# The first 128 tokens of block 0 sent ahead in a four-stage transformer kernel, with the table of steps laid anew

## The reference

```python
x = x + attn(ln(x))    # 16 heads of 8 dims over 1024 keys; + input; LayerNorm with gamma, beta
x = x + ffn(ln(x))     # ternary weights: silu(x W1) * (x W2), two 512x512 GELU layers, then W3
x = x + gla(ln(x))     # gated linear attention: h = h * exp(gk) + k v^T, o = q h over T
x = x + zones(ln(x))   # router takes 3 of 8 expert FFNs (128 -> 512 -> 128) per batch
...
Q = x @ wq + bq; K = x @ wk + bk; V = x @ wv + bv
Q = Q.reshape(B * H, S, D); K = K.reshape(B * H, S, D); V = V.reshape(B * H, S, D)
attn = softmax(einsum('bqd,bkd->bqk', Q, K) / sqrt(D))
```

## Time and profile before

| | us |
|---|---|
| median of 3 runs (1034.36 to 1039.66) | 1035.55 |
| the profiled execution: its time | 1037.2 |
| the profiled execution: its span | 1034.9 |
| PE busy | 966.3 (93%) |
| ACT busy | 813.3 (79%) |
| DVE busy | 720.5 (70%) |
| POOL busy | 356.4 (34%) |
| first exponential (ACT L909) starts at | 28.18 |

### The profile page before, as it was taken

One profiled execution on the slowest core, in us unless ns is written; L12 is line 12 of the kernel. 1 busy time (PEld: TensorE's weight loads), 2 busy tenths in 40 slices (PEclk: granted clock), 3 DMA queues, 4 the chain that ended last, 5 costly groups with the idle time before them and its releaser, 6 DMA issues.

```text
span 1034.9 us, 16677 instructions
## 1 busy us (share of the span) xinstructions
PE 966.3 (93%) x5859; PEld 454.0 (44%) x5859; DVE 720.5 (70%) x1276; ACT 813.3 (79%) x1058; POOL 356.4 (34%) x309
## 2 busy tenths in 40 slices
PE   3999999999999999999999998999899999999998
PEld 1232235333533452346233533453347666566666
DVE  5223855567488778777888887688699998997300
ACT  0899888988889989999899898989976485644542
POOL 1000102114322435343625342534554465546100
PEclk8899999999999999999999999999999999999999
DMA  6855244065216533651266136412342322252020
GB/s 158 194 145 139 72 122 116 32 141 148 62 61 166 134 81 92 147 146 58 62 157 171 53 93 179 128 43 75 92 105 82 97 84 82 74 145 68 12 71 21
DMA packets 140998, 106.26 MB, mean 103 GB/s; under 512 B 92848, under 2 KB 107984, under 8 KB 140880
## 3 DMA queue, kind: packets, MB, share of 16 engines
q1 hardware_dynamic: 135984, 102.78, 37.3%
q10 hardware_dynamic: 4896, 1.87, 0.7%
HBM read 75.25 MB, written 29.36 MB: 101 GB/s over the span
## 4 chain that ended last, share of the span: by engine, by line
PE 47%; ACT 16%; DVE 16%; issue 11%; DMA 4%; POOL 4%; SPq 1%; ACTq 0%; DVEq 0%; POOLq 0%
PE PS L1488 14%; ACT R L909 9%; PE PS L1451 9%; PE PS L1535 7%; DVE R L1264 4%; DVE R L1255 4%; PE PS L1662 4%; DMA R<-VD 3%; ACT L883 3%; PE PS L1650 3%; PE PS L1575 2%; PE PS L1597 2%; PE PS L1606 1%; POOL R L854 1%; DVE RB L1220 1%
## 5 line engine op out<-in xcount | busy, mean ns | idle before, releaser
L909 ACT ACTIVATE R<-PS 128x1024 f32<-128x1024 f32 x512 | 487.2, 1042 | 55.9 <-PE PS L1451 54.2
L1488 PE MATMUL PS<-R 128*32 128x512 f32 x2048 | 293.5, 611 | 1.0 <-DVE R L1208 0.9
L854 POOL TENSOR_TENSOR R<-R 128x512 f32<-128x512 f32 x128 | 189.8, 1489 | 185.5 <-ACT R L985 126.0
L1451 PE MATMUL PS<-RA 32*128 32x512 f32 x1024 | 181.3, 500 | 29.0 <-ACT R L909 23.4
L1264 DVE TENSOR_TENSOR_SCAN R<-R 128x512 f32<-128x512 f32 x128 | 186.0, 1453 | 2.3
L1451 PEld LDWEIGHTS PS<-RA 32*128 32x128 f32 x1024 | 70.6, 183 | 255.3 <-ACT R L909 164.4
L1535 PE MATMUL PS<-RB,WR 128*128 128x512 f32 x640 | 175.7, 416 | 5.3 <-POOL RB L840 2.7
L1535 PEld LDWEIGHTS PS<-RB,WR 128*128 128x128 f32 x640 | 115.3, 189 | 69.0 <-issue 29.5
L883 ACT ACT_TABLE_LOAD x84 | 107.8, 1283 | 35.6 <-PE PS L1535 12.8
L1255 DVE TENSOR_TENSOR R<-R 128x512 f32<-128x512 f32 x128 | 118.5, 926 | 22.7 <-DMA R<-VD 18.5
L840 POOL TENSOR_TENSOR RB<-R,RB 128x512 fp32r<-128x512 f32 x48 | 74.9, 1560 | 164.6 <-DVE RB L1220 164.6
(11 more groups left out here) (127 smaller groups left out, 856.6 us busy)
## 6 DMA issues: line engine op xcount, KB each, us to landing
R<-VD SPq DMA_DIRECT2D x128, 256.0 KB, 4.1
RA<-QD SPq DMA_DIRECT2D x64, 256.0 KB, 4.4
QD<-RA SPq DMA_DIRECT2D x56, 256.0 KB, 3.9
RA<-QD SPq DMA_DIRECT2D x64, 128.0 KB, 4.3
OD<-R SPq DMA_DIRECT2D x32, 256.0 KB, 2.1
R<-OD SPq DMA_DIRECT2D x128, 32.0 KB, 2.5
R<-in_Wa SPq DMA_DIRECT2D x12, 256.0 KB, 3.7
R<-in_Wb SPq DMA_DIRECT2D x12, 256.0 KB, 4.2
```

Source lines behind the costliest of these rows:

```text
L854: pool.tensor_tensor(st, st, Qc, ALU.mult).then_inc(S["qh"], 1)
L909: act.activation(PR[u % 4], bank(2 * s, 1024), ACT.Exp, scale=SC).then_inc(S["exp"], 1)
L1451: op = pe.matmul(bank(2 * s + h), exact(KS[k][p:p + 32, 128 * j:128 * j + 128]), exact(QS[k][p:p + 32, :]), start=True, stop=stop)
L1488: op = pe.matmul(bank(ob)[c:c + 32, :], VAF[b % 2][:, at:at + 32], PR[u % 4][:, 512 * h:512 * h + 512], start=(j == 0), stop=(j == 7), til ...
```

## The change

Block 0 is treated in two parts, `(0, 0, 1)`, its first 128 tokens, and `(0, 1, 4)`, the other 384. x comes in two DMAs accordingly. The first part's K goes out by SP, its Q by ACT's DMA queue, and the first pair's keys are read by SP and its queries by ACT. The weights wA and the bias bA are asked for by ACT (in two halves), ahead of bv, gsel and block 1's x; the x of blocks 2 to 7 is asked for by SP after pair 2. For all blocks, `hi` is rounded straight from PSUM with the bias (DVE L1153; by ACT L937 for block 0's Q) and `lo` is formed straight from PSUM (L1157), so there is no Qf, one DVE instruction less, and the bank is given back after `lo`; the magnitude is taken of `hi`, and the limit is lowered by 2^-9 for that. PE's `values` waits for wA's second half (bv_in). POOL's `shift` waits for its own last instruction instead of a semaphore. The steps of block 1 no longer stand ahead of the first scores, and the string is another one, of the same length and with the same count of each letter.

```diff
-    "qqqqwxxxxxxxxxxxqxxxxxxlxxxxxxxxxxxxxxxwxwxxwxlxxxxxxwxxxfxxxqxxwfxwxxlxxwqqxwxxwxxxxxlxxwxxxxxfwxxx"
+    "xxxxxxxxxxxxqxxwxqxxqxxxxqxxxxxxwxxwxxxlxxfwxxxwqxxxxxxxxxwxwqxxlxxwxxxqxlqwxxxxxfxxxlwxxxwwfxxpxxxx"
...
     def start(self):
-        e = self.norm_in(0)
-        self.add("pads", 0)
-        self.add("turn_in", 0, 1, e)
-        self.add("split", 0, 1, 2)
-        self.add("keep", 0, 1, 0, 1)
-        self.add("split", 0, 0, 3)
-        self.add("keep", 0, 0, 0, 1)
-        self.add("load_pair", 0)
+        first, rest = (0, 0, 1), (0, 1, 4)
+        for k in range(2):
+            self.add("pads", k)
+        e = {}
+        n = self.stats("q", "X", first, ("x_in0", 16))
+        e[first] = self.apply("q", "XN", "X", first, n)
+        n = self.stats("q", "X", rest, ("x_rest", 16))
+        self.add("turn_in", first, 1, e[first])
+        e[rest] = self.apply("q", "XN", "X", rest, n)
+        self.add("split", first, 1, 2)
+        self.add("split", first, 0, 3)
+        self.add("first_out", 1)
+        self.add("first_out", 0)
+        self.add("turn_in", rest, 0, e[rest])
+        self.add("split", rest, 1, 4)
+        self.add("split", rest, 0, 5)
+        self.add("first_pair", 1)
+        self.add("first_pair", 0)
+        self.add("values", 0, 1)
+        self.add("flag", 0, 2)
         for w in (1, 0):
             self.add("keep", 0, w, 1, 4)
         for n in (1, 2):
             self.add("load_pair", n)
-        self.add("values", 0, 4)
-        self.add("flag", 0, 5)
-        self.add("pads", 1)
+        self.add("inputs")
         self.add("late_loads")
-        self.add("attend")
...
+        def keep_first(engine, need, w, landed):
+            need.wait_ge("qk_parts", split_no(0, 0, w))
+            for i in range(2):
+                for copy in range(2):
+                    engine.dma_start(place(0, w, 0, 1, i, copy), words(Qp[w][:, i, 0:128])).then_inc(S[landed], 16)
...
-            sp.dma_start(xblock(0), x_v[:, 0:4, :]).then_inc(S["x_in0"], 16)
-            sp.dma_start(wA[:, :, :], io["wA"]).then_inc(S["small_in"], 16)
-            sp.dma_start(bA[:, :], io["bA"]).then_inc(S["small_in"], 16)
+            sp.dma_start(X[:, 0:1, :], x_v[:, 0:1, :]).then_inc(S["x_in0"], 16)
+            sp.dma_start(X[:, 1:4, :], x_v[:, 1:4, :]).then_inc(S["x_rest"], 16)
...
+            def first_out(w):
+                if w:
+                    keep_first(sp, need, w, "k_out0")
+
+            def first_pair(w):
+                if w:
+                    need.wait_ge("k_out0", 64)
+                    keys(0, 0, "pair_in0")
+
+            def inputs():
+                for b in range(2, NBLK):
+                    sp.dma_start(xblock(b), x_v[:, 4 * b:4 * b + 4, :]).then_inc(S["x_in%d" % b], 16)
...
             def shift(k, n):
                 i = LNS[k]
-                need.wait_ge("rstd_" + k, n)
...
+            act.dma_start(wA[:, 0:2, :], io["wA"][:, 0:2, :]).then_inc(S["small_in"], 16)
+            act.dma_start(bA[:, :], io["bA"]).then_inc(S["small_in"], 16)
+            act.dma_start(wA[:, 2:4, :], io["wA"][:, 2:4, :]).then_inc(S["bv_in"], 16)
             for c in range(2):
                 act.dma_start(bv2[64 * c:64 * c + 64, :, :],
                               bass.AP(io["bv"].tensor, 8 * c, [[0, 64], [16, 8], [1, 8]])).then_inc(S["bv_in"], 16)
             act.dma_start(gsel[:, :], io["gsel"]).then_inc(S["ones"], 16)
-            for b in range(1, NBLK):
-                act.dma_start(xblock(b), x_v[:, 4 * b:4 * b + 4, :]).then_inc(S["x_in%d" % b], 16)
+            act.dma_start(xblock(1), x_v[:, 4:8, :]).then_inc(S["x_in1"], 16)
...
+            def split(part, w, bk):
+                b, i0, i1 = part
+                if b == 0 and w == 0:
+                    need.wait_ge("qk_ps", split_no(b, i0, w))
+                    need.wait_ge("small_in", 32)
+                    act.activation(exact(Qp[0][:, 0, 128 * i0:128 * i1]), bank(bk)[:, 128 * i0:128 * i1], ACT.Identity,
+                                   bias=bA[:, 0:1]).then_inc(S["q_hi"], 1)
+
+            def first_out(w):
+                if w == 0:
+                    keep_first(act, need, w, "q_out0")
+
+            def first_pair(w):
+                if w == 0:
+                    need.wait_ge("q_out0", 64)
+                    queries(act, 0, 0, "pair_in0")
...
-            def split(b, w, bk):
-                n = split_no(b, w)
-                hi, lo = Qp[w][:, 0, :], Qp[w][:, 1, :]
+            def turn_in(part, bk, e):
+                b, i0, i1 = part
+                need.wait_ge("xt_ps", turn_no(b, i0))
+                dve.tensor_copy(xtblock(b)[:, 128 * i0:128 * i1], bank(bk)[:, 128 * i0:128 * i1]).then_inc(S["xt"], 1)
+
+            def split(part, w, bk):
+                b, i0, i1 = part
+                n = split_no(b, i0, w)
+                ps = bank(bk)[:, 128 * i0:128 * i1]
+                hi, lo = (exact(Qp[w][:, i, 128 * i0:128 * i1]) for i in range(2))
                 need.wait_ge("qk_ps", n)
                 need.wait_ge("small_in", 32)
-                if n > 1:
-                    need.wait_ge("amax", n - 1)
-                    need.wait_ge("qk_parts", n - 1)
-                dve.tensor_scalar(Qf, bank(bk), bA[:, w:w + 1], None, ALU.add).then_inc(S["qk_f"], 1)
-                need.wait_ge("qk_f", n)
                 if b:
                     need.wait_ge("k_out" if w else "q_out", 64 * b)
-                    need.wait_ge("qk_out0", 128)
-                own.step(dve.tensor_copy(exact(hi), Qf))
-                own.settle()
-                dve.tensor_tensor(exact(lo), Qf, exact(hi), ALU.subtract).then_inc(S["qk_parts"], 1)
-                dve.tensor_reduce(am[:, 2 * b + w:2 * b + w + 1], Qf, AX.X, ALU.max,
+                    need.wait_ge("k_out0" if w else "q_out0", 64)
+                    need.wait_ge("amax", 2 * b - w)
+                if b or w:
+                    own.step(dve.tensor_scalar(hi, ps, bA[:, w:w + 1], None, ALU.add))
+                    own.settle()
+                else:
+                    need.wait_ge("q_hi", 2 if i0 else 1)
+                dve.scalar_tensor_tensor(lo, ps, bA[:, w:w + 1], hi, ALU.add, ALU.subtract).then_inc(S["qk_parts"], 1)
+                if b:
+                    largest(b, w)
+                elif i0 and w == 0:
+                    largest(0, 1)
+                    largest(0, 0)
+
+            def largest(b, w):
+                dve.tensor_reduce(am[:, 2 * b + w:2 * b + w + 1], words(Qp[w][:, 0, :]), AX.X, ALU.max,
                                   apply_absolute_value=True).then_inc(S["amax"], 1)
...
-                emptied[bk] = ("qk_f", split_no(b, w))
+                need.wait_ge("xt", turn_no(b, i0))
+                room(bk)
+                pe.matmul(bank(bk)[:, 128 * i0:128 * i1], wA[:, w, :], xtblock(b)[:, 128 * i0:128 * i1], start=True,
+                          stop=True).then_inc(S["qk_ps"], 1)
+                emptied[bk] = ("qk_parts", split_no(b, i0, w))
 
             def values(b, bk):
-                need.wait_ge("small_in", 32)
-                need.wait_ge("xt", b + 1)
+                need.wait_ge("bv_in", 48)
+                need.wait_ge("xt", b + 2)
```

167 lines of the change are left out of this document (83 added, 84 removed).

## The result

The changed kernel took **1011.3 us** (median of 4, 1009.61 to 1013.15) where the kernel before, measured beside it, took 1035.9: a ratio of 0.974, interval [0.971, 0.978], 24.6 us less. The forecast was 1029.3, in 1021 to 1037: the sign was right, and the gain was about four times as large. A second series of the changed kernel (e18) gave 1012.6 (ratio 0.978 [0.975, 0.980]).

What follows compares the result with a forecast made beforehand. PE and ACT together were taken to pace the long middle. The terms 6.6 - 1.6 + 4.9 - 2.6 - 0.9 gave 6.4 us less, 1030.8 against the profiled 1037.2, so 1029.3 as median; range 1021 to 1037.

Steps and rivals of the forecast that it cites:

- the long middle keeps its pace: From 100 to 764 us: condition for carrying the earlier start to the end, with PE and ACT pacing together.
- The new start: Ahead of the first scores: first exponential at 21.6, 6.6 us earlier; 9.7 or 4.0 earlier if gsel lands early or late.
- carried to the end: Whole span: whatever brings the first scores forward reaches the end, counted at the full 6.6 us.
- Block 1 out of the hole: Block 1's transposes and one projection move from PE's idle time in among the scores: 1.6 us lost, 0 to 3.2.
- Table loads: Ahead of the last exponential: 59 become 48, 1.283 us each, 35% on the chain; 4.9 us gained, bounds 0 and 14.1.
- PE's 94% in the middle leaves it little to give: From 100 to 764 us: argument for a rival in which the early start is not carried, 1035 us, chance 0.23.
- DVE's split, x by SP, POOL's shift: Blocks 1 to 7's split saves 6.0 us of DVE, covered by idle time; x's loads come early enough; all taken as 0.
- The end: After the last exponential: three more products and scans, 2.6 us lost, and three more table loads, 0.9 lost.
- C: Rival: early start not carried, gsel late, loads off the chain; 0 to 2 us slower or the same, 1035; chance 0.23.
- D: Rival: from 764 to 960 us DVE waits for replicas at its products (R<-VD); slower, 1041 to 1044 us; chance 0.12.
- B: Rival: gsel lands early and the removed loads were nearly all on the chain; 13.6 us less, 1022; chance 0.2.

Runs made afterwards that it cites:

- e18: The changed kernel once more, unchanged, as a second series; 1012.6 us, ratio 0.978 [0.975, 0.980].
- e1: The changed kernel with the string of the kernel before, all else new; 1035.2 us, ratio 1.000 [0.999, 1.002].
- e2: The kernel before with only the new string put in; 1014.0 us, ratio 0.980 [0.976, 0.984].
- e10: The kernel before with the FFN's GELU computed as tanh, table loads 84 to 37, nothing moved; 1036.2 us, ratio 1.000 [0.997, 1.003].
- e11: The changed kernel with the FFN's GELU computed as tanh, table loads 76 to 38, nothing moved; 1010.0 us, ratio 0.972 [0.968, 0.976].
- e3: The changed kernel with the new string's first 88 letters, up to the 64th x, then the old string; 1032.4 us, ratio 0.997 [0.994, 0.999].
- e8: The changed kernel with the scores of each pair's first two units multiplied twice, 128 matmuls more; 1008.9 us, ratio 0.971 [0.968, 0.974].
- e5: The kernel before with GELU letters drawn together at ten places of its string, table loads 84 to 62; 1059.5 us, ratio 1.018 [1.014, 1.023].
- e6: The changed kernel with GELU letters drawn together at six places of its string, table loads 76 to 64; 1025.3 us, ratio 0.988 [0.985, 0.991].
- e9: The kernel before with only x letters moved out of ten GELU groups, table loads 84 to 62; 1053.5 us, ratio 1.013 [1.007, 1.018].
- e12: The changed kernel with only x letters moved behind five GELU groups, table loads 76 to 66; 1023.8 us, ratio 0.985 [0.981, 0.989].
- e7: The changed kernel with reloads of the already loaded table ahead of eleven pairs' first exponentials, 8 loads more; 1023.4 us, ratio 0.984 [0.980, 0.988].
- e4: The kernel before with hi and lo formed straight from PSUM, without Qf, old start and string; 1034.2 us, ratio 0.998 [0.997, 1.000].

## Why the prediction was wrong

**The step that failed** is the one that took the string into the sum by its table loads alone, 4.9 us. All else that a new order does was put at nothing without a reason: the prediction asked only that "the long middle keeps its pace". It did not keep it. The order by itself is worth 24 of the 25 us (e1, e2), and 19.0 us of the stretch between the exponentials with the loads made equal (e10, e11); the loads' own part is nothing that can be told from the noise.

**The new start (6.6 us earlier): the number right, partly by luck.** Foretold 21.6, found 21.59. gsel, issued at 3.63 as said, landed after 5.9 us and not 7.8, so L930 ran at 9.53 and ACT's writes of Q were issued from 10.47 and not from 12.15. That lead was lost again, as the last of the four writes took long:

```profile
L667 ACTq DMA_DIRECT2D QD<-RA x4: 386/491/505, 10.5 to 11.9; - x4
...
DMA to landing us min/median/max: 1.7/1.8/4.1
```

The landings are those of all eight such writes, SP's four and ACT's. ACT's last one took the 4.1 us and landed at 16.0, where 1.7 us was counted. The second read was issued at 16.6 and landed at 20.2, and the scores started at 20.76, where 20.7 was said. The two misses cancelled. The flag (18.14) was 2 us early. That the start would be **carried to the end** was right only in part: 2.7 us of 5.3 by e1 and e3, and the clock's falls are shown to have taken most of the rest in one pair of executions.

**Block 1 out of the hole (1.6 lost):** its transposes stand at 37.02 among the scores and take 0.66 us instead of 1.09. Their cost is not seen apart; e8 suggests that such work beside exponentials is free.

**Table loads (4.9 gained): wrong.** I took the loads' share of the chain, 35%, as what a load gives back when it goes. Their share did fall as said, from 3.9% of 664 us to 1.8% of 637:

```profile
by line: PE PS L1546 19.6%; PE PS L1593 13.1%; PE PS L1509 13.1%; ACT R L956 13.1%; issue 10.9%; PE PS L1655 4.3%; PE PS L1633 2.9%; PE PS L1664 2.8%; DMA R<-VD 2.6%; ACT L916 1.8%; DVE R L1322 1.5%; DVE R L1313 1.4%; PE PS L1448 1.1%; PE P
```

Still 47 gone loads gave 1.4 us by the levels, no more than its own uncertainty (e10), and fewer loads made by closer GELUs went with 9 to 14 us more (e5, e6, e9, e12). The chain names an engine's work wherever it passes; it does not say that another chain of the same length doesn't run beside it.

**"PE's 94% in the middle leaves it little to give": the reading that hid the gain.** Busy is there the time in which any matmul is in flight, waiting ones too: the new string took 8.6 us out of it with the same work, and 11.5 out of the idle time. The doses show the room: 14 us free in the scores, about full price in the FFN. So PE paces the FFN, and beside the doubled scores something else does: by e7's full price for ACT's work at such places it is ACT. That the new string gains by evening out the waits between the two fits this: PE waits 15.6 us for the exponentials instead of 23.4 and the exponentials 38.2 us for scores instead of 54.2 (7.9 of it at the first exponential). What in the new string brings that about is not shown.

**DVE's split, x by SP, POOL's shift (0):** for the split e4 gives 1 to 2 us, which is near what can be told. The other two were not run apart; e1 has them all, and it is no faster than the kernel before.

**The end (3.5 lost):** from the last exponential to the end of the last scan 186.9 us before (764.3 to 951.2) and 189.2 now (737.5 to 926.7), 2.3 more, where 3.5 were counted (2.6 and 0.9); behind the scan it is 2.1 us shorter (83.7, 81.6).

**The rivals.** C was right that loads were changed against waits and that the start is not all carried, and wrong on what PE has to give. D did not come: behind the last exponential R<-VD has 6.4% of the chain (737 to 927), 12 us, where it had 23 before. Over the whole kernel, though, R<-VD grew from 18.5 to 26.6 us of DVE's idle time ahead of these products, and all of that idle time from 22.7 to 27.5; no run here prices it. B's size was nearer, for a cause that e10 and e11 exclude. None had the interleaving as a gain of its own: with a string that was laid anew over 1800 letters, one was owed, and a range that reached it.

## What to carry to other kernels

Where two engines take turns as the pacing one, give neither a price from its share of the span or of the chain: put a dose of work on it, or take one away, in each kind of stretch, and read what the end does. A change of the order of issue over the whole program is a change of its own, often larger than the edit that it comes with; run each with the other's partner before explaining either. And note the mean clock beside each time: here 0.010 of it went with some 7 us, though not in every kernel. Last, when a whole class of work is suspected, take it out of both kernels and see whether the difference stays, as e10 and e11 do.

## What the chip showed that I had not expected

- The falls of the granted clock come at other places in each execution and take back a lead: the same 288 matmuls took 51.70 us at 0.97 and 54.82 at 0.91.
- Executions with 14 us of unneeded PE matmuls beside the first scores had a mean granted clock of 0.992, without them 0.987, and were 2 to 4 us faster. Which fall they prevent was not looked for, and in e1 the executions with the highest mean clock were the slowest, so a mean clock alone does not give the time.
- e5, e6 and e9, in which the GELUs stand together, had a lower clock in their means (0.976, 0.981, 0.981): by the slope above about a third of what their medians lost is clock.
- A load of the function table costs 1.28 us with no drain on either side of it (0.02 us to the next activation), and 47 of them could go without a gain.
